# A graph network's expert stage: second weights in 4 KB pieces, first biases read once, empty tiles spread, and the router's residual products moved into the edge sums

## What is computed

```
m  = segment_sum(h[src], dst) * rsqrt(deg_in)
xr = (m @ W_gc + b_gc) + (feats @ W_res + b_res)
logits = xr @ Wg + bg;  vals, idx = top_k(logits, 2);  gates = softmax(vals)
h1 = gelu(xr_rows @ w1[e] + b1[e])          # w1[e] 256 x 512
h2 = h1 @ w2[e] + b2[e]                     # w2[e] 512 x 256
y  = xr + sum over the two of gate * h2;  batch norm over nodes
```

## Time and profile before

| | |
|---|---|
| median of 3 runs | 6748.72 us (6743.35 to 6772.54) |
| profiled execution, its own time | 6708.42 us |
| its span | 6706.8 us |
| PE, DVE, ACT, POOL busy | 65%, 52%, 33%, 48% of the span |
| granted TensorE clock, mean | 0.78 |
| edge sums, routing with its tail, experts | about 1306, 219 and 589 us |

### The profile page before, as it was taken

The page is one execution under the profiler, slowest core; times in us unless marked ns, Lnnn a source line. Parts: engine busy times, 40 slices in busy tenths (PEclk is TensorE's granted clock), DMA queues, the critical chain, the costliest instruction groups (busy, mean ns, idle before and its releaser), DMA issues. The chain is left out here.

```text
span 6706.8 us, 90264 instructions
## 1 busy us (share of the span) xinstructions
PE 4342.6 (65%) x24913; PEld 3150.9 (47%) x24913; DVE 3458.5 (52%) x6689; ACT 2184.9 (33%) x7656; POOL 3192.9 (48%) x3187
## 2 busy tenths in 40 slices
PE   6996676766677744544444546887646666666676
PEld 4664454544445423333333435766335555555553
DVE  4452666666666662211111231112558888888885
ACT  1221455555545430000000111222225454555541
POOL 0422566666666236676676520002145565655551
PEclk8896777777777876666766778998778888888885
DMA  4334666666666525333333407882366666666673
GB/s 133 126 123 163 182 197 199 202 196 198 198 196 197 125 72 186 93 93 93 92 95 92 72 29 243 261 262 87 108 189 205 203 210 203 205 207 203 201 185 102
DMA packets 509932, 1077.03 MB, mean 161 GB/s; under 512 B 94770, under 2 KB 322388, under 8 KB 505993
## 3 DMA queue, kind: packets, MB, share of 16 engines
q0 software_dynamic: 204144, 617.42, 32.6%
q1 hardware_dynamic: 296854, 452.03, 20.2%
q10 hardware_dynamic: 8512, 2.74, 0.2%
HBM read 964.49 MB, written 194.54 MB: 173 GB/s over the span
## 5 line engine op out<-in xcount | busy, mean ns | idle before, releaser
L772 POOL DMA_INDIRECT l0e_kv<-t_table,k_recs x912 | 986.1, 1081 | 636.9 <-ACT l0e_vw L1049 375.5
L772 POOL DMA_INDIRECT l3e_kv<-t_table,k_recs x912 | 971.0, 1065 | 667.5 <-ACT l3e_vw L1049 368.0
L1464 PE MATMUL l2e_pA<-l2e_row,l2e_oh 128*128 128x257 f32 x1824 | 633.4, 516 | 768.7 <-issue 380.4
L1418 POOL DMA_INDIRECT l2e_row<-t_table,l2e_idx x912 | 899.7, 986 | 389.7 <-issue 265.4
L1464 PEld LDWEIGHTS l2e_pA<-l2e_row,l2e_oh 128*128 128x128 f32 x1824 | 460.0, 262 | 942.0 <-issue 852.9
L1006 PE MATMUL l0e_pA<-l0e_vw,l0e_ohf 128*128 128x260 f32 x1824 | 643.9, 500 | 198.3 <-ACT l0e_vw L1049 129.2
L958 PE MATMUL l3e_pQE<-l3e_qb,l3e_ohT 128*128 128x256 bf16 x2736 | 428.0, 318 | 405.9 <-issue 378.7
L1049 ACT ACTIVATE l3e_vw<-l3e_kv,l3e_w 128x64 f32<-128x64 f32 x2736 | 679.8, 334 | 0.0
L1049 ACT ACTIVATE l0e_vw<-l0e_kv,l0e_w 128x64 f32<-128x64 f32 x2736 | 679.6, 334 | 0.0
L1443 DVE SCALAR_TENSOR_TENSOR l2e_acc<-l2e_acc,k_itf,l2e_pA 128x257 f32<-128x257 f32 x228 | 109.9, 482 | 1058.6 <-issue 981.9
L1006 PEld LDWEIGHTS l0e_pA<-l0e_vw,l0e_ohf 128*128 128x128 f32 x1824 | 427.7, 247 | 338.5 <-ACT l0e_vw L1049 156.6
(11 more groups left out here) (469 smaller groups left out, 7126.8 us busy)
## 6 DMA issues: line engine op xcount, KB each, us to landing
exp_w<-in_L_gnn_w SPq DMA_DIRECT2D x224, 512.0 KB
t_table<-l0n_tab SPq DMA_DIRECT2D x26, 2048.0 KB, 6.9
l0e_qb<-t_q SPq DMA_DIRECT2D x228, 192.0 KB
l3e_qb<-t_q SPq DMA_DIRECT2D x228, 192.0 KB
t_agg<-l0e_acc SPq DMA_DIRECT2D x228, 130.0 KB
t_agg<-l3e_acc SPq DMA_DIRECT2D x228, 130.0 KB
l0e_drow<-t_drow SPq DMA_DIRECT2D x57, 512.0 KB
l3e_drow<-t_drow SPq DMA_DIRECT2D x57, 512.0 KB
```

Of the source, the lines that this page charges most:

```text
L772: pool.indirect_dma_start(kv[:, n % SK, g, :], None, table[:, :], bass.IndirectOffsetOnAxis(ap=K["recs"][:, n, g, ridx:ridx + 1], axis=0)) ...
L1418: pool.indirect_dma_start(row[:, s, g, 0:D], None, table[:, :], bass.IndirectOffsetOnAxis(ap=idx[:, i, g:g + 1], axis=0)).then_inc(row_rea ...
L1464: last = pe.matmul(pA[s % 2][:, 0:W], oh[:, s, g, :], row[:, s, g, :], start=(g == 0), stop=(g == G - 1))
```

## The change

- Experts: `w2` is read as `(p c) n`, 128 pieces of 4 KB, so partition p holds hidden units 4p to 4p + 3. To match, the hidden product loads columns m, m + 4, m + 8, ... of `w1`, and b1 has the same order.
- The first biases of all 64 experts are read in one DMA in the edge sums into a buffer that stays; DVE reads the tile's expert to a register and copies four columns. PE's transpose of b1 and the DMA for each tile go.
- Tile `i + u * 14` takes the place of `i * 8 + u`. The first turn's loads aren't conditional any more.
- Routing: the products of `h2` with `W_res`, their transposes and the sum of the two biases are done in the edge sums, one block after every 8 items from item 8 on; routing adds its own product to them.

```diff
@@ sum_items
+        def tile_of(i, late):
+            t, r = divmod(i - late - EVERY, EVERY)        # EVERY = 8
+            return t if r == 0 and 0 <= t < NBP else None
 DVE, item i:
+                if i == EVERY:
+                    dve.wait_ge(next_in, 16 * 6)
+                    dve.tensor_tensor(bias[:, 0, :], bias[:, 0, :], bias[:, 1, :], ALU.add).then_inc(bias_ready, 1)
+                    dve.wait_ge(bias_ready, 1)
                 add(i)
+                t = tile_of(i, 4)
+                if t is not None:
+                    dve.wait_ge(r_ps, t + 1)
+                    dve.tensor_tensor(xx[:, t, :], pR[:, 0:D], bias[:, 0, :], ALU.add).then_inc(r_ready, 1)
 PE, behind the products of item i:
+                t = tile_of(i, 0)
...
+                        last = pe.transpose(pT[:, c, :], h2[:, t, c * P:(c + 1) * P], K["ident"][:, :])
+                t = tile_of(i, 2)
...
+                        last = pe.matmul(pR[:, 0:D], hT[:, t % 2, c, :], wr[:, 2 + c, :], start=(c == 0), stop=(c == 1))
 ACT, behind the copy of item i:
+                t = tile_of(i, 1)
...
+                    act.activation(hT[:, t % 2, :, :], pT[:, 0:2, :], ACT.Copy).then_inc(hT_ready, 1)
 SP, between bias and bg:
+            sp.dma_start(M["b1"][:, :, :], A["L2_gnn_b1"].rearrange("e (p m) -> p e m", m=HID // P)).then_inc(b1_in, 16)
@@ route
-            dve.tensor_tensor(bias[:, 0, :], bias[:, 0, :], bias[:, 1, :], ALU.add)
-                dve.tensor_tensor(xx[:, t, :], pXX[t % 2][:, 0:D], bias[:, 0, :], ALU.add).then_inc(xx_ready, 1)
+                dve.tensor_tensor(xx[:, t, :], pXX[t % 2][:, 0:D], xx[:, t, :], ALU.add).then_inc(xx_ready, 1)
-                for c in range(4):       # turn and residual
+                for c in range(2):
@@ experts, SP
-                e = sp.value_load(K["tiles"][0:1, 0, bass.ds(i * U + u, 1)], min_val=0, max_val=EX - 1)
+                e = sp.value_load(K["tiles"][0:1, 0, bass.ds(i + u * TURNS, 1)], min_val=0, max_val=EX - 1)
+                only = {} if isinstance(i, int) and i == 0 else {"cond": live}
-                sp.dma_start(w2[:, u, :, :], A["L2_gnn_w2"][bass.ds(e, 1), :, :].rearrange("e (c p) n -> p (e c) n", p=P), cond=live).then_inc(w_in[u], 16)
-                sp.dma_start(b1[:, u, :], A["L2_gnn_b1"][bass.ds(e, 1), :].rearrange("e (m p) -> (e m) p", p=P)).then_inc(w_in[u], 16)
+                sp.dma_start(w2[:, u, :, :], A["L2_gnn_w2"][bass.ds(e, 1), :, :].rearrange("e (p c) n -> p (e c) n", c=HC), **only).then_inc(w_in[u], 16)
@@ experts, PE
-                pe.wait_ge(w_in[u], snap(pe, (i + 1) * 80))
+                pe.wait_ge(w_in[u], snap(pe, (i + 1) * 64))
-                pe.transpose(pX[u % 2][:, 2, 0:HC], b1[:, u, :], K["ident"][0:HC, 0:HC]).then_inc(x_ps, 1)
-                        last = pe.matmul(pH[u % 2][:, m, :], w1[:, u, c, m * P:(m + 1) * P], xT[:, u, c, :], start=(c == 0), stop=(c == 1))
+                        last = pe.matmul(pH[u % 2][:, m, :], w1[:, u, c, bass.ds(m, P, HC)], xT[:, u, c, :], start=(c == 0), stop=(c == 1))
@@ experts, DVE
+                e = dve.value_load(K["tiles"][0:1, 0, bass.ds(i + u * TURNS, 1)], min_val=0, max_val=EX - 1)
+                need(dve, h_ready, i - 1, u)
+                dve.tensor_copy(b1T[:, u, :], b1[:, bass.ds(e, 1), :].rearrange("p e m -> p (e m)"))
                 need(dve, x_ps, i, u)
-                need(dve, h_ready, i - 1, u)
-                dve.tensor_copy(b1T[:, u, :], pX[u % 2][:, 2, 0:HC])
                 dve.tensor_copy(xT[:, u, :, :], pX[u % 2][:, 0:2, :]).then_inc(xT_ready, 1)
```

More of the change, by code:

```diff
@@ L1395, in sum_items @@
         acc = S.sb("acc", [P, SL, W])
-        all_agg = M["agg"]
+        all_agg, xx, h2, wr, bias = M["agg"], M["xx"], M["h2"], M["w"], M["bias"]
+        hT = S.sb("hT", [P, 2, 2, P])
+        pT = S.ps("pT", [P, 4, P])
+        pR = S.ps("pR", [P, 512])
+        bias_ready, hT_ps, hT_ready, r_ps, r_ready = (S.sem(k) for k in ("bias_ready", "hT_ps", "hT_ready", "r_ps", "r_ready"))
+        EVERY = 8
         pA = [S.ps(f"pA{j}", [P, 512]) for j in range(2)]
@@ L1399, in sum_items @@
         row_ready, oh_ready, a_ps, item_done, filed = (many(k) for k in ("row_ready", "oh_ready", "a_ps", "item_done", "filed"))
-        consts, idx_ready, dl_done, next_in, cleared = (S.sem(k) for k in ("consts", "idx_ready", "dl_done", "next_in", "cleared"))
+        consts, idx_ready, dl_done, next_in, cleared, b1_in = (S.sem(k) for k in ("consts", "idx_ready", "dl_done", "next_in", "cleared", "b1_in"))
         block = S.block()
@@ L1465, in _ @@
                 last.then_inc(a_ps[s], 1)
+                t = tile_of(i, 0)
+                if t is not None:
+                    if t:
+                        pe.wait_ge(hT_ready, t)
+                    for c in range(2):
+                        last = pe.transpose(pT[:, c, :], h2[:, t, c * P:(c + 1) * P], K["ident"][:, :])
+                    last.then_inc(hT_ps, 1)
+                t = tile_of(i, 2)
+                if t is not None:
+                    if t == 0:
+                        pe.wait_ge(next_in, 16 * 6)
+                    pe.wait_ge(hT_ready, t + 1)
+                    if t:
+                        pe.wait_ge(r_ready, t)
+                    for c in range(2):
+                        last = pe.matmul(pR[:, 0:D], hT[:, t % 2, c, :], wr[:, 2 + c, :], start=(c == 0), stop=(c == 1))
+                    last.then_inc(r_ps, 1)
         @block.scalar
@@ L1476, in _ @@
                 last.then_inc(filed[s], 1)
+                t = tile_of(i, 1)
+                if t is not None:
+                    act.wait_ge(hT_ps, t + 1)
+                    if t >= 2:
+                        act.wait_ge(r_ps, t - 1)
+                    act.activation(hT[:, t % 2, :, :], pT[:, 0:2, :], ACT.Copy).then_inc(hT_ready, 1)
         @block.sync
@@ L1489, in _ @@
             sp.wait_ge(cleared, 16)
+            sp.wait_ge(b1_in, 16)
 def route(nc, A, T, K, M):
@@ L1498, in route @@
         mh = S.sb("mh", [P, 2, D])
-        mT = S.sb("mT", [P, 2, 4, P])
+        mT = S.sb("mT", [P, 2, 2, P])
         xT = S.sb("xT", [P, 2, 2, P])
@@ L1694, in turned @@
                     act.wait_ge(xx_ps, t - 1)
-                act.activation(mT[:, t % 2, :, :].rearrange("p c k -> p (c k)"), pT[t % 2][:, :], ACT.Copy).then_inc(mT_ready, 1)
+                act.activation(mT[:, t % 2, :, :].rearrange("p c k -> p (c k)"), pT[t % 2][:, 0:2 * P], ACT.Copy).then_inc(mT_ready, 1)
             def turned_xx(t):
@@ L1716, in turn @@
                     pe.wait_ge(mT_ready, t - 1)
-                for c in range(4):
-                    x = mh[:, t % 2, c * P:(c + 1) * P] if c < 2 else h2[:, t, (c - 2) * P:(c - 1) * P]
-                    last = pe.transpose(pT[t % 2][:, c * P:(c + 1) * P], x, K["ident"][:, :])
+                for c in range(2):
+                    last = pe.transpose(pT[t % 2][:, c * P:(c + 1) * P], mh[:, t % 2, c * P:(c + 1) * P], K["ident"][:, :])
                 last.then_inc(t_ps, 1)
@@ L1725, in residual @@
                     pe.wait_ge(xx_ready, t - 1)
-                for c in range(4):
-                    last = pe.matmul(pXX[t % 2][:, 0:D], mT[:, t % 2, c, :], w[:, c, :], start=(c == 0), stop=(c == 3))
+                for c in range(2):
+                    last = pe.matmul(pXX[t % 2][:, 0:D], mT[:, t % 2, c, :], w[:, c, :], start=(c == 0), stop=(c == 1))
                 last.then_inc(xx_ps, 1)
@@ L1772, in _, with experts @@
             pe.matmul(pTiles[0:1, 0:NTILE], K["ones"][0:EX, 0:1], jf[:, :], start=True, stop=True).then_inc(base_ps, 1)
-def experts(nc, A, T, K):
+def experts(nc, A, T, K, M):
     with Stage(nc, "exp") as S:
@@ L1779, in experts @@
         U = 8
+        TURNS = NTILE // U
         w1 = S.sb("w1", [P, U, 2, HID])
         w2 = S.sb("w2", [P, U, HC, D])
-        b1 = S.sb("b1", [HC, U, P])
+        b1 = M["b1"]
         b2 = S.sb("b2", [P, U, D])
@@ L1808, in load @@
             def load(i, u):
-                e = sp.value_load(K["tiles"][0:1, 0, bass.ds(i * U + u, 1)], min_val=0, max_val=EX - 1)
-                live = sp.value_load(K["tiles"][0:1, 1, bass.ds(i * U + u, 1)], min_val=0, max_val=1)
+                e = sp.value_load(K["tiles"][0:1, 0, bass.ds(i + u * TURNS, 1)], min_val=0, max_val=EX - 1)
+                live = sp.value_load(K["tiles"][0:1, 1, bass.ds(i + u * TURNS, 1)], min_val=0, max_val=1)
+                only = {} if isinstance(i, int) and i == 0 else {"cond": live}
                 need(sp, y_ready, i - 1, u)
                 sp.sem_inc(turn, 1)
-                sp.dma_start(w1[:, u, :, :], A["L2_gnn_w1"][bass.ds(e, 1), :, :].rearrange("e (p c) n -> p (e c) n", c=2), cond=live).then_inc(w_in[u], 16)
-                sp.dma_start(w2[:, u, :, :], A["L2_gnn_w2"][bass.ds(e, 1), :, :].rearrange("e (c p) n -> p (e c) n", p=P), cond=live).then_inc(w_in[u], 16)
-                sp.dma_start(x[:, u, :], rows(T["xslot"], snap(sp, (i * U + u) * P)), cond=live).then_inc(w_in[u], 16)
```

(18 more changed lines are left out.)

## The result

| kernel | median, us | range, us | runs |
|---|---|---|---|
| before | 6746.03 | 6739.58 to 6772.54 | 4 |
| after | 6807.84 | 6800.65 to 6814.29 | 4 |

The ratio of after to before is 1.0082, with a 95% interval from 1.0056 to 1.0107: the kernel is slower, by 61.8 us or 0.8%. The forecast was 6819 us, slower by 70. The profiled execution of after took 6814.29 us (span 6812.7) at a mean granted clock of 0.779.

The account below looks back on a forecast made before the run. The prediction took SP's issuing to bound the experts, PE close behind, routing one chain per tile and edge sums POOL's. Terms 93 - 29 + 6 = +70 us on the 6748.7 us median gave 6819 us, range 6650 to 6885.

Parts of the forecast that it names:

- The step decides, and PE becomes the bound: Experts: w1's step of 4 floats raises a pass from 0.111 to 0.23 us, putting PE above SP's 4.85 us.
- B: Rival, experts: a pass costs 0.256 us, 47 us more, 6866 us; chance 0.58 together with the main forecast.
- A tile of 5.84 us: Experts, PE's time per tile: 16 passes at 0.23, 1.63 for the result, 0.53 for turning x.
- Wraps: Experts: at 13 wraps to a new turn PE waits 1.24 us, DVE's fetch taken at 0.84; 16 us.
- Experts 683 us, +93: Experts stage: 13 + 112 x 5.84 + 16 = 683 us against 589, less 1 for the shorter first load.
- b1's load: Experts: dropping each tile's b1 load saves SP 0.55 us, 62 us over 112 tiles.
- rival A: Experts: the step is free and SP stays the bound; experts win 66 us, kernel 6660 us; chance 0.24.
- w2's pieces: Experts: 4 KB pieces of w2 may save SP 0.05 us of issue on 89 tiles, 4 us.
- Spreading: Experts: spreading empty tiles leaves SP's sum unchanged; worth 3 us only where PE is slower, counted as 0.
- Routing -29 us: Routing: two transposes and four passes leave each tile's chain, 1.03 us x 26 = 27, 29 with half-clock first tiles.
- Edge sums +6 us: Edge sums: moved PE work 10 us at most, b1's 16-byte pieces 0 to 13; 6 taken for both.
- rival C: Experts: PE's clock falls; at 1.2 GHz +235 us, 7054 us, a third of it likelier; chance 0.05.

Follow-up runs that it names:

- e1: After with the hidden product loading 128 neighbouring w1 columns again, w2 still in 4 KB pieces; 6648.89 us, ratio to before 0.9838.
- e2: Before with only the step of 4 floats in w1 and w2 in 4 KB pieces added; 6866.32 us, ratio to before 1.0158.
- e5: After with a step of 2 floats instead of 4 in the hidden product's w1 loads; 6654.4 us, one execution.
- e7: After with a step of 8 floats instead of 4 in the hidden product's w1 loads; 6827.95 us, one execution.
- e3: After with the whole experts stage of before, keeping the changed routing and edge sums; 6730.54 us, ratio to before 0.9957.
- e9: e4 with the tiles in their old order, empty ones last; 6610.45 us, ratio to before 0.986.
- e4: After with neighbouring w1 columns, w2 in 1 KB pieces, b1 loaded as 1 KB rows and turned once on the chip; 6643.44 us, ratio to before 0.9831.
- e8: e4 with finished tiles stored from ACT's queue instead of SP's, two tiles late; 6602.35 us, ratio to before 0.9771.
- e6: After with a step of 3 floats instead of 4 in the hidden product's w1 loads; 6715.77 us, one execution.

## Why the prediction was right, step by step

- *The step decides, and PE becomes the bound.* Right, shown by e1 and e2. I said 0.23 us a pass; it is 0.2325. e5 to e7 show the reason given, groups of 16 bytes, and not distance or latency alone. B's 0.256 came from 64 bf16 columns with a step of 52 bytes; e7 shows that for these passes a wider step adds only 2%.
- *A tile of 5.84 us.* It is 5.68. The term that was off is the turn of x: I had kept the 0.53 of the trace of before, which is the distance to the start of b1's transpose. With that transpose gone, the next group starts after 0.32. That is 0.21 x 112 = 24 us too much, against 4 too little for the passes.
- *Wraps.* 13 times 1.24 forecast, 13 times 1.65 measured in the weight loads (21.2 us; PE's matmuls show 18.8). A turn of 8 tiles takes 47.08 us (4294.96 to 4342.04), 1.64 more than 8 x 5.68. The fetch of the tile's number isn't all of it. After first, a copy of b1 by DVE inside a turn, then PE's turning and DVE's copy at a wrap; below it the same at a wrap of before:

```profile
4305.69 0.17 DVE L1939 COPY exp_b1T<-moe_b 128x4 f32 x1 [0.51 <-issue]
...
4339.75 0.65 PEld L1891 LDWEIGHTS exp_pX<-k_ident,exp_x 128*128 128x128 f32 x4
...
4341.44 0.17 DVE L1939 COPY exp_b1T<-moe_b 128x4 f32 x1 [0.79 <-issue]
```

```profile
4535.68 0.41 PEld L1850 LDWEIGHTS exp_pX<-k_ident,exp_x 128*128 128x128 f32 x2
...
4536.77 0.16 DVE L1898 COPY exp_b1T<-exp_pX 128x4 f32<-128x4 f32 x1 [0.18 <-issue]
...
4536.80 0.13 PEld L1851 LDWEIGHTS exp_pX<-k_ident,exp_b 4*128 4x128 f32 x1
```

  At the wrap DVE's issue grew from 0.18 to 0.79 us, so the fetch adds 0.61, within the 0.84 allowed. The other 0.6 was missing from the forecast: PE's turning ahead of the wrap shrank from 1.25 us (4535.68 to 4536.93), with two transposes of b1 in it, to 0.65. PE waits for DVE there, so what left PE's program came back as waiting: 0.39 + 0.61 + 0.60 = 1.60.

- *Experts 683 us, +93.* They are 675.9 between marks that give before 594.1: +82. The 5.68 a tile, the wraps, and 19 us of head and tail, where I had allowed 13, add up to it (636 + 21 + 19 = 676). Against e3, which has before's experts and 589.3, it is +87.
- *b1's load.* Mis-sized: 0.55 us a tile forecast, 0.82 to 0.90 measured in e9. I read the distance from its issue to the next issue, but the address work ahead of it goes as well. In after this has no effect, as PE covers it. With the 11 us of spreading it is why e1 came to 89 us less in the experts, where rival A had 66: 78 for b1's load instead of 62, 11 for spreading instead of 0, and none of the 4 for w2's pieces.
- *w2's pieces.* 4 us forecast, 0 measured (e1 and e4). *Spreading* was counted at 0. In after nothing tests that; against e9, e4 shows 11 us, where I had allowed 3, since the sum took 3.94 us of PE against 3.8 of SP for the empty tiles, and it is 3.75, with 1.64 at each wrap, against 3.44.
- *Routing -29 us.* Measured -28, by the earlier trace rows to the term: 1.03 x 26 forecast, 1.08 (4.07 to 2.99) measured.
- *Edge sums +6 us.* Not to be told from 0: 1309.3 and 1320.5 us without the added work, 1319.8, 1320.3, 1321.4, 1319.7 and 1309.5 with it. PE's 26 blocks were covered. Two figures beside the forecast are slightly off in their own sums and enter nothing: 26 x 2.1 is 55 and not 57, and SP's mean step (589 - 13 - 66) / 112 is 4.55 and not 4.56.
- *The sum.* +70 forecast, +62 by the timed runs. Experts and routing alone give +54 (82 - 28), or +59 against e3's experts; the last 3 to 8 us are within what one trace differs from the next. That the total came so near is in part luck: the turn of x (24 us too much) was partly offset by the passes (4), the wraps (5) and head and tail (6), all too small. The clock, on which rival C rested, was 0.96.

## What to carry to other kernels

A larger DMA piece isn't free if it decides the layout that an engine reads: weigh the piece against the step that it forces on the operands, and count the 16-byte groups that a weight load touches (64 for 128 fp32 columns cost next to nothing here, 128 doubled the pass). Find who issues before asking how many bytes move: over the whole experts' stage the same loads ran at 222 GB/s in before, 263 in e4 and 288 in e8, as SP had less and less to issue. When an operand is used with a new step, look for a row of the profile that already has that step on the same engine; twice the 0.115 us of the x transposes gave the price of a pass to 1%.

## What the runs showed of the hardware

- A pass of 128 fp32 weight columns cost 0.112 (e1), 0.119 (e5), 0.174 (e6), 0.2325 (after) and 0.236 us (e7) at steps of 1, 2, 3, 4 and 8 floats, all at a granted clock of 0.96 to 0.98.
- One small load in SP's loop over tiles cost 0.8 to 0.9 us of SP, though its issue shows as 0.31 us. With all four loads turned off by their condition, a step of four loads and a store still took 3.4 us (e1, e9).
- With w2 in pieces of 1 KB (e4) or of 4 KB (e1), the experts' stage moved 263 GB/s, with the DMA engines busy for 0.82 and 0.80 of it. SP set the pace in both, so this isn't a comparison of the transfers themselves.
- A register fetch on DVE ahead of a small copy added 0.61 us at a wrap, where PE waited for it, and nothing that shows inside a turn.
